# Two position buffers, masks ahead of their copies, later constants' products and evenly spread normalisations in a graph-and-experts layer

## The reference, cut to what matters

```python
xn = _layernorm(x)                                   # normalised rows
messages = xn[dst] * edge_weight[:, None]            # edge_index = [src, dst]
agg = segment_sum(messages, src, num_segments=6250)  # what needs the edges by source row
h = relu((xn + agg) @ W1 + b1)
x = x + h @ W2 + b2 + mix(xn)                        # mix: 8 heads, k^T v, then q (k^T v), + xn
x = x + ffn(_layernorm(x))                           # top 2 of 16 experts, then layernorm
```

## Time and profile before

| what | value |
|---|---|
| median of 3 runs | 1928.92 us (1926.7 to 1930.55) |
| the profiled execution's own time | 1930.95 us |
| its span in the profile | 1929.2 us |
| PE busy | 1718.8 us, 89% of the span |
| DVE busy | 1308.9 us, 68% |
| POOL busy | 1142.4 us, 59% |
| ACT busy | 735.7 us, 38% |
| mean granted clock of TensorE | 0.947 of full speed |

### The profile page before, as it was taken

One profiled execution on the slowest core, in us unless ns is written; L12 is line 12 of the kernel. 1 busy time (PEld: TensorE's weight loads), 2 busy tenths in 40 slices (PEclk: granted clock), 3 DMA queues, 4 the chain that ended last, 5 costly groups with the idle time before them and its releaser, 6 DMA issues. The chain is left out here.

```text
span 1929.2 us, 42450 instructions
## 1 busy us (share of the span) xinstructions
PE 1718.8 (89%) x11804; PEld 1551.2 (80%) x11804; DVE 1308.9 (68%) x3885; ACT 735.7 (38%) x2167; POOL 1142.4 (59%) x1172
## 2 busy tenths in 40 slices
PE   6249997679989999999999999999679999999976
PEld 5149997568878888888888888888569999999964
DVE  6889997589966777777776777676435555555546
ACT  4758995001002333333333333332323333333347
POOL 0005556677777777777777777777125555555524
PEclk9569999689999999999999999999789999999989
DMA  6001110454434444444444444444246522222258
GB/s 186 0 1 44 43 43 25 146 161 137 140 111 130 130 129 129 131 130 130 126 132 125 129 127 131 129 130 126 96 137 209 172 72 70 73 72 72 70 175 312
DMA packets 126831, 223.38 MB, mean 116 GB/s; under 512 B 24987, under 2 KB 81547, under 8 KB 126522
## 3 DMA queue, kind: packets, MB, share of 16 engines
q0 software_dynamic: 52928, 135.73, 23.8%
q1 hardware_dynamic: 46026, 59.55, 9.4%
q10 hardware_dynamic: 27696, 25.83, 4.2%
HBM read 178.67 MB, written 42.35 MB: 115 GB/s over the span
## 5 line engine op out<-in xcount | busy, mean ns | idle before, releaser
L1384 POOL DMA_INDIRECT lower<-xn_rows,lower x792 | 765.6, 967 | 241.4 <-issue 220.7
L1549 DVE TENSOR_SCALAR lower<-bank,lower 128x128 f32<-128x128 f32 x888 | 320.1, 402 | 66.9 <-issue 48.7
L1409 PE MATMUL bank<-ones,ident 128*128 128x128 f32 x2084 | 284.4, 279 | 20.1 <-DVE xh L1566 13.5
L1409 PEld LDWEIGHTS bank<-ones,ident 128*128 128x128 f32 x2084 | 272.5, 194 | 32.3 <-DVE xh L1566 14.7
L1425 PE MATMUL bank<-lower 128*128 x888 | 269.3, 385 | 9.3 <-SPq L1254 5.3
L1426 PE MATMUL bank<-lower 128*128 x888 | 265.3, 380 | 0.0
L1566 DVE TENSOR_TENSOR xh<-xh,bank 128x256 f32 x444 | 183.4, 413 | 120.5 <-PE bank L1426 119.9
L612 POOL DMA_INDIRECT edge_records_sorted<-lower x112 | 113.6, 1014 | 217.6 <-ACT lower L802 167.0
L2055 DVE TENSOR_SCALAR arena<-bank,b_tile 128x128 f32<-128x128 f32 x456 | 128.3, 344 | 165.3 <-PE bank L1928 165.3
L1928 PEld LDWEIGHTS bank<-arena 128*128 128x128 f32 x1824 | 224.3, 194 | 13.7 <-ACT arena L1983 8.0
L1928 PE MATMUL bank<-arena 128*128 128x128 f32 x1824 | 225.2, 277 | 7.3 <-ACT arena L1983 7.3
(11 more groups left out here) (368 smaller groups left out, 2496.0 us busy)
## 6 DMA issues: line engine op xcount, KB each, us to landing
lower<-xn_rows,lower POOLq DMA_INDIRECT x792
lower<-in_L_ffn_w SPq DMA_DIRECT2D x16, 512.0 KB
upper<-in_L_ffn_w SPq DMA_DIRECT2D x16, 512.0 KB
xn_rows<-xh SPq DMA_DIRECT2D x7, 896.0 KB, 4.5
lower<-xn_rows ACTq DMA_DIRECT2D x49, 128.0 KB
xn_rows<-lower ACTq DMA_DIRECT2D x49, 128.0 KB
x_plus_beta<-lower ACTq DMA_DIRECT2D x49, 128.0 KB
upper<-in_x SPq DMA_DIRECT2D x1, 6144.0 KB
```

Of the source, the lines that this page charges most:

```text
L1384: pool.indirect_dma_start(edge_rows[:, t % ROUND, :], None, xn_dram, bass.IndirectOffsetOnAxis(source.bitcast(U32)[:, t:t + 1], 0)).then_i ...
L1409: pe.matmul(sums_at(u)[:, 0:P], ident[:], ones[:], start=True, stop=True)
L1549: dve.tensor_scalar(edge_sel[:, (2 * u + h) % ESEL, :], iota_gather, lane[:, at:at + 1], weight_s[:, at:at + 1], ALU.is_equal, ALU.mult).t ...
```

## The change

Four things are done, all in the first stage.

1. There are two position buffers, and copies write them in turn. Both are set to zero first, and each copy waits for the copy two before it. At the end the buffers are added into the first one. Every edge has exactly one bucket, so one of the two is zero.
2. The 14 masks that are made again are made two at a time, ahead of five copies of kept buckets and then the two copies that read them. The waits for the masks themselves are gone; the wait for the copy two before covers them.
3. The 24 products of constants wait for the shifts (`s_shift`) in place of ACT's sums.
4. ACT normalises two tiles behind the weights of each of the first three groups of a round and one behind the fourth, and does so before it copies PE's result, in place of three and four tiles behind the copies of two groups.

```diff
-        pos = carve(EC // 2).bitcast(U16)
-        part_i = carve(EC).bitcast(I32)
+        pos = [carve(EC // 2).bitcast(U16) for _ in range(2)]
         masks = [carve(EC // 2).bitcast(U16) for _ in range(4)]
+        part_i = last_match[:, EC // 2:EC // 2 + EC].bitcast(I32)
...
-            pe.wait_ge(s_sums, (NG - 1) * 2 * GT)
+            pe.wait_ge(s_shift, 1)
             for k in range(24):
                 pe.matmul(bank[4][:, 0:P], ident[:], ones[:], start=True, stop=True)
...
             def rounds(r):
                 weights(r, 0)
+                norm(r, range(0, 2))
                 if looped(r) or r >= 1:
                     copy_across(r - 1, GPR - 1)
                     copy_quads(r - 1, GPR - 2)
-                norm(r, range(0, GT // 2))
                 weights(r, 1)
+                norm(r, range(2, 4))
                 copy_across(r, 0)
                 if looped(r) or r >= 1:
                     copy_quads(r - 1, GPR - 1)
-                norm(r, range(GT // 2, GT))
                 weights(r, 2)
+                norm(r, range(4, 6))
                 copy_across(r, 1)
                 copy_quads(r, 0)
                 weights(r, 3)
+                norm(r, range(6, GT))
                 copy_across(r, 2)
                 copy_quads(r, 1)
...
-            masked = copied = None
-            for r in KEPT + tuple(r for r in range(NR) if r not in KEPT):
-                for i in range(GT):
-                    b = r * GT + i
-                    if r in KEPT:
-                        mask = match[r][:, i * EC:(i + 1) * EC].bitcast(U16)
-                    else:
-                        mask = masks[b % 4]
-                        dve.tensor_scalar(mask, bkt_c, iota_n[:, b:b + 1], None, ALU.is_equal).then_inc(s_dve, 1)
-                        masked = n.add()
-                        dve.wait_ge(s_dve, masked)
-                        dve.sem_inc(s_apart, 1)
-                    if copied:
-                        dve.wait_ge(s_dve, copied)
-                        dve.sem_inc(s_apart, 1)
-                    dve.copy_predicated(columns(pos), columns(mask), start[:, b * NGRP:(b + 1) * NGRP].unsqueeze(1)
-                                        .to_broadcast([P, GC, NGRP])).then_inc(s_dve, 1)
-                    copied = n.add()
+            for a in pos:
+                dve.memset(a, 0).then_inc(s_dve, 1)
+            memset = n.add(2)
+            made = [b for b in range(NT) if b // GT not in KEPT]
+            held = [b for b in range(NT) if b // GT in KEPT]
+            PAIR, HELD = 2, len(held) * 2 // len(made)
+            copied = [memset, memset]
+
+            def copy(b, mask):
+                dve.wait_ge(s_dve, copied[-2])
+                dve.sem_inc(s_apart, 1)
+                dve.copy_predicated(columns(pos[len(copied) % 2]), columns(mask),
+                                    start[:, b * NGRP:(b + 1) * NGRP].unsqueeze(1).to_broadcast([P, GC, NGRP])).then_inc(s_dve, 1)
+                copied.append(n.add())
+
+            for k in range(len(made) // PAIR):
+                for b, mask in zip(made[k * PAIR:(k + 1) * PAIR], masks[k % 2 * PAIR:]):
+                    dve.tensor_scalar(mask, bkt_c, iota_n[:, b:b + 1], None, ALU.is_equal).then_inc(s_dve, 1)
+                n.add(PAIR)
+                for b in held[k * HELD:(k + 1) * HELD]:
+                    copy(b, match[b // GT][:, b % GT * EC:(b % GT + 1) * EC].bitcast(U16))
+                for b, mask in zip(made[k * PAIR:(k + 1) * PAIR], masks[k % 2 * PAIR:]):
+                    copy(b, mask)
+            dve.wait_ge(s_dve, n.back(0))
+            dve.tensor_tensor(pos[0], pos[0], pos[1], ALU.add).then_inc(s_dve, 1)
+            dve.wait_ge(s_dve, n.add())
```

More of the change, by code:

```diff
@@ new lines, in edges_vector @@
+            memset = n.add(2)
+            made = [b for b in range(NT) if b // GT not in KEPT]
+            held = [b for b in range(NT) if b // GT in KEPT]
+            PAIR, HELD = 2, len(held) * 2 // len(made)
+            assert len(made) % PAIR == 0 and len(held) * PAIR == HELD * len(made)
+            copied = [memset, memset]
[5 more added lines that the diff above has]
+                copied.append(n.add())
@@ L953, in edges_vector @@
                 cols = slice(h * GC // 2, (h + 1) * GC // 2)
-                dve.tensor_tensor(by_column(pos_i)[:, cols, :], columns(pos)[:, cols, :],
+                dve.tensor_tensor(by_column(pos_i)[:, cols, :], columns(pos[0])[:, cols, :],
                                   bank[6 + h][:, 0:EH].rearrange("p (j g) -> p j g", g=NGRP), ALU.add).then_inc(s_dve, 1)
```

## The result

The changed kernel takes 1911.96 us (median of 4 runs, 1911.15 to 1912.75) against 1929.6 us for the kernel before (median of 4, 1926.7 to 1930.55): ratio 0.9909, 95% interval [0.9896, 0.9922], 17.6 us less. The profiled execution took 1912.67 us, its span is 1910.8 us. The forecast was 1912.3.

The account below looks back on a forecast made before the run. DVE's lookups were taken to bound the time up to the first group, PE's products the sort after it. 11.5 - 0.2 + 2.7 + 2.6 = 16.6 us off 1928.9 gave 1912.3 us, range 1909 to 1922.

Parts of the forecast that it names:

- Part 1: DVE's lookups: copies in two buffers and masks made ahead take 49.7 us against 61.2, so 11.5 us less.
- The step that carried it: DVE's lookups: a copy waiting for the copy two before it starts like a non-waiting mask, pitch 0.89 us instead of 1.12.
- The addition: End of DVE's lookups: adding the two buffers of 784 16-bit values, taken at 0.55 us, between 0.54 and 0.95.
- The rule of the Trainium skill: DVE's chained copies: the next operation can't start before the pipeline empties, so the lookups' gain would be next to nothing.
- the mask at 96.63: DVE's lookups before the change: a mask that waits for nothing, starting 0.89 us behind a copy's start, 0.09 before its end.
- Part 2: PE ahead of the sort: constants' products start with the shifts, so the first group takes 6.33 us; 2.7 gained, 0.2 lost.
- The 0.2: PE's first group: the moved products end late, so it starts at about 120.8 instead of 120.6 us.
- The sum: Whole kernel: 11.5 - 0.2 + 2.7 + 2.6 = 16.6 us less, giving 1912.3 us.
- Part 3: ACT in the sort: at most two normalisations a group bring the pitch to 6.74 us throughout, 2.6 us gained.
- My reason for it: ACT in the sort: two normalisations keep it under 6.74 us a group, placed ahead of the result's copy where ACT waited.
- The earlier end: End of the sort: the first gather waits for the scatter's last transfer, so an earlier end is passed on whole.
- The room at ACT's root: Behind the lookups: the reciprocal moves to 111.4 us, ACT's root ends at 110.51, so a microsecond of room is left.

Follow-up runs that it names:

- p1_lookups_only: Kernel before with only the lookups changed (two buffers, masks ahead), plus gather counts masked to 12 bits; 1920.42 us, ratio 0.9960 to the kernel before.
- q1_wait_for_last: a0_after with each copy waiting for the copy just before it instead of two before; 1923.70 us, ratio 0.9976 to the kernel before.
- q2_three_pairs: a0_after with three pairs of satisfied wait and increment ahead of each copy instead of one; 1913.22 us, ratio 0.9926 to the kernel before.
- a0_after: The changed kernel plus gather counts masked to 12 bits; 1914.27 us, ratio 0.9925 to the kernel before.
- p2_products_only: Kernel before with only the 24 constants' products waiting for the shifts, plus gather counts masked to 12 bits; 1927.26 us, ratio 0.9996 to the kernel before.
- q4_norms_behind: a0_after with the same two, two, two and one normalisations placed behind the copies of PE's results; 1913.89 us, ratio 0.9927 to the kernel before.
- v1_early_masks: a0_after with the two fills and first four remade masks moved ahead of DVE's wait for SP's totals; 1913.36 us, ratio 0.9916 to the kernel before.
- b0_before: Kernel before plus gather counts masked to 12 bits, base for the single-part kernels; 1929.86 us, ratio 1.0010 to the kernel before.

## Why the prediction was right

**Part 1.** Forecast 49.7 us for the lookups and 11.5 gained; measured 49.4 and 11.78. It is also the only part whose gain the times show by themselves (p1_lookups_only and q1_wait_for_last). The step that carried it, that a copy whose wait is satisfied follows as the unwaiting mask does after 0.89 us, was right twice: by the pitch in the changed kernel (0.88) and by q2_three_pairs. The addition took 0.57 us, for which I had 0.55 between 0.54 and 0.95. The rule of the Trainium skill that was weighed there (page "VectorE: DVE Perf Modes", section "The DRAIN you can't avoid": chained copies take the same time with a semaphore after each as with one after the last) doesn't carry over to these copies, each of which waits for the one before: q1_wait_for_last and a0_after differ in which copy is waited for and in nothing else, and the lookups differ by 10.4 us. The prediction read that section by halves. It also says that a next operation that is not held starts earlier, and the mask at 96.63 and the copies 0.88 us apart in the changed kernel agree with that.

**Part 2.** Forecast 0.2 lost at the first group and 2.7 gained behind it; measured 0 and 2.93 in the pair of profiles. The mechanism was right: PE comes to the first group at the full clock. The 0.2 did not come, because the products were out of the way when the row mask was ready (PE still waits 0.27 us for it in the changed kernel, 0.72 in p2_products_only). The second group follows 6.55 us after the first and not 6.74 as I had put it: the pitch in mid sort holds a transposition (`L733`), and ahead of the second group there is none. The size of the rest was a lucky draw: what the products save is what a cold first group loses, and that was 9.27, 7.90, 8.88, 8.27 and 8.56 us in five executions against 6.33 warm, so 1.6 to 2.9 us. The sum took the one value that the profile before showed, as if it were fixed.

**Part 3.** Forecast 2.6 us, measured 2.46 to 2.49 in every one of the kernels that carry it; a pitch of 6.745 instead of 6.74 is the difference. My reason for it was half right: the spread is what counts. That the normalisations stand ahead of the copy of the result, which I had counted on as a use of ACT's waiting time, gives nothing (q4_norms_behind).

**The rest.** The earlier end was passed on: 17.45 us at the last group, 17.29 at the first gather. The room at ACT's root, which I had put at a microsecond, is 0.66 us in the changed kernel (the root ends at 110.16, the reciprocal starts at 110.82); v1_early_masks ran into it.

**The number.** Forecast 16.6 us less and 1912.3 us, measured 17.6 less (15.1 to 20.1 by the interval) and 1911.96. That the medians agree within 0.4 us is luck. Read from the rows, the parts give 11.7, 1.6 to 2.9 and 2.5 us, together 15.7 to 17.1, depending on how long a cold first group happens to take. The other pair, b0_before and a0_after, whose cold group took 7.90, differs by 15.33 us at the last group and by 15.6 in the medians.

## What to carry to other kernels

When operations of one engine must follow one another through the same buffer, look at what an independent instruction does behind the same operation in the trace: the gap between the two pitches, 1.12 and 0.88 us here, is what a second buffer is worth, times the number of operations that stand directly behind another of them (42 of the 49 here: 42 x 0.24 = 10.1 us, measured 10.4). Warm-up products were worth something here only directly ahead of the work that they warm up; ten microseconds earlier they bought nothing. And an engine with room on average can still set the pace where its work comes in lumps: compare its work per step, not per round, with the pace of the engine that it feeds.

## What the hardware showed unexpectedly

- The same cold products took from 7.00 to 8.39 us for 48 rows in different executions, and the first cold group 7.90 to 9.27, and the time until the clock rises differs with them. The kernel before and b0_before started their first group at 132.12 and 132.16; the granted clock was 0.50 up to 138 us in the one, and 0.65 between 134 and 136 and 1.00 from 136 on in the other.
- A pause of a few microseconds gave the clock away. In the kernel before and in p1_lookups_only PE's products ended at 110.06 and 110.16, and the granted clock was 1.00 up to 114 and 0.50 from 115 us on, so that the first group began at the lower level in both.
- Two further satisfied waits and increments ahead of each of 49 copies cost DVE nothing that the trace shows (6.28 us for seven copies with one pair and with three).
- A predicated copy of 784 16-bit values takes 0.98 us, and the next instruction starts after 0.88 to 0.89 if it need not wait for it, after 1.12 if it must.
